# A fused Perceiver block: order of loads and vector work in cross attention, and five value products moved into latent attention's head

## The reference

```python
x = x + cross_attention(layernorm(x), ctx_2048, mask)   # scores over 256 context rows of the same sequence
x = x + latent_attention(layernorm(x), weights)         # 16 heads, low-rank queries (384) and keys/values (128), rotary part (64)
x = x + ffn(layernorm(x), weights)                      # 2048 wide, squared relu, plus one dense "expert" product, layernorm
```

## Time and profile before

| | |
|---|---|
| median of 3 runs | 1130.35 us (1129.69 to 1131.27) |
| the profiled execution | 1130.65 us |
| span of its instructions | 1128.8 us |
| PE busy | 1093.4 us, 97% |
| PEld busy | 950.7 us, 84% |
| DVE busy | 533.0 us, 47% |
| ACT busy | 353.0 us, 31% |
| POOL busy | 323.0 us, 29% |

### The profile page before, as it was taken

One profiled execution on the slowest core, in us unless ns is written; L12 is line 12 of the kernel. 1 busy time (PEld: TensorE's weight loads), 2 busy tenths in 40 slices (PEclk: granted clock), 3 DMA queues, 4 the chain that ended last, 5 costly groups with the idle time before them and its releaser, 6 DMA issues.

```text
span 1128.8 us, 20917 instructions
## 1 busy us (share of the span) xinstructions
PE 1093.4 (97%) x8097; PEld 950.7 (84%) x8097; DVE 533.0 (47%) x998; ACT 353.0 (31%) x699; POOL 323.0 (29%) x370
## 2 busy tenths in 40 slices
PE   5999999999999999999999999999999999999996
PEld 2667686898888888898888888989899998989895
DVE  3666566445344443445344446746254443525242
ACT  3465655232222323232222225513131221213130
POOL 2243362121212112120212122436142332425151
PEclk9899999999999999999999999999999999999998
DMA  9999921101111110201111116501010010101000
GB/s 361 418 420 418 419 91 51 42 20 41 51 42 56 42 46 19 79 19 37 51 42 56 37 49 201 202 1 39 1 38 18 21 38 0 37 0 38 1 19 19
DMA packets 41279, 100.96 MB, mean 89 GB/s; under 512 B 7497, under 2 KB 11620, under 8 KB 36740
## 3 DMA queue, kind: packets, MB, share of 16 engines
q1 hardware_dynamic: 41220, 100.16, 24.7%
HBM read 74.45 MB, written 17.30 MB: 81 GB/s over the span
## 4 chain that ended last, share of the span: by engine, by line
PE 89%; DMA 3%; DVE 3%; issue 2%; POOL 1%; SPq 1%; ACT 1%; DVEq 0%; POOLq 0%; ACTq 0%
PE b_z L44 6%; PE b_z L45 6%; PE b_z L46 6%; PE b_score L44 5%; PE b_prob L44 5%; PE b_prob L46 5%; PE b_score L46 5%; PE b_score L45 5%; PE b_prob L45 5%; PE b_z L1077 3%; PE b_turn L44 2%; PE b_read L608 2%; PE b_read L44 2%; PE b_free L44 2%; PE b_read L46 2%; PE b_free L46 2%
## 5 line engine op out<-in xcount | busy, mean ns | idle before, releaser
L808 POOL TENSOR_TENSOR m_e<-m_e,m_rs 128x512 f32<-128x512 f32 x32 | 34.7, 1085 | 358.2 <-DVE m_rs L955 358.2
L1407 POOL TENSOR_TENSOR f_hT_lo<-f_h,f_hT_hi 128x512 fp32r<-128x512 f32 x64 | 89.6, 1399 | 94.2 <-ACT f_hT_hi L1450 89.5
L46 PE MATMUL b_z<-m_zT_hi,m_wq_hi 128*128 128x256 f32 x384 | 108.7, 283 | 0.0
L44 PE MATMUL b_z<-m_zT_lo,m_wq_hi 128*128 128x256 f32 x384 | 108.7, 283 | 0.0
L45 PE MATMUL b_z<-m_zT_hi,m_wq_lo 128*128 128x256 f32 x384 | 108.7, 283 | 0.0
L1506 DVE TENSOR_TENSOR f_h<-f_h 128x512 f32<-128x512 f32 x64 | 70.6, 1104 | 61.5 <-ACT f_h L1445 61.5
L896 DVE TENSOR_TENSOR m_pT_lo<-b_turn,m_pT_hi 128x512 fp32r<-128x512 f32 x32 | 22.1, 692 | 160.4 <-ACT m_pT_hi L855 160.4
L849 ACT ACTIVATE m_qT<-b_z,m_q_bias 128x256 f32<-128x256 f32 x128 | 53.8, 472 | 79.1 <-PE b_z L46 75.4
L44 PEld LDWEIGHTS b_z<-m_zT_lo,m_wq_hi 128*128 128x128 f32 x384 | 73.7, 192 | 0.0
L45 PEld LDWEIGHTS b_z<-m_zT_hi,m_wq_lo 128*128 128x128 f32 x384 | 73.7, 192 | 0.0
L46 PEld LDWEIGHTS b_z<-m_zT_hi,m_wq_hi 128*128 128x128 f32 x384 | 73.7, 192 | 0.0
(11 more groups left out here) (222 smaller groups left out, 3161.6 us busy)
## 6 DMA issues: line engine op xcount, KB each, us to landing
x_ctx_in<-ctx_rows_dram SPq DMA_DIRECT2D x16, 1024.0 KB, 11.2
x_ctxT<-ctx_turned_dram SPq DMA_DIRECT2D x15, 1024.0 KB, 10.8
m_swapped<-m_by_sin SPq DMA_DIRECT2D x128, 64.0 KB, 2.0
z_scratch<-x_zbuf SPq DMA_DIRECT2D x16, 288.0 KB, 9.7
m_raw<-attn_raw_dram SPq DMA_DIRECT2D x6, 768.0 KB, 11.7
m_z_in<-z_scratch SPq DMA_DIRECT2D x8, 576.0 KB, 3.8
x_x_all<-x_dram SPq DMA_DIRECT2D x16, 256.0 KB, 10.5
x_scratch<-x_x_all SPq DMA_DIRECT2D x16, 256.0 KB, 11.0
```

The costliest lines, as they stand in the source:

```text
L44: nc.tensor.matmul(out, lh, rl, start=first, stop=False)
L46: return nc.tensor.matmul(out, lh, rh, start=False, stop=last)
L808: q.tensor_tensor(e[:], e[:], rs[:].unsqueeze(2).broadcast_to([P, HB, SEQ]), ALU.mult).then_inc(s["normed"], 1)
L1407: g.tensor_tensor(hT_lo[:, 2 * n:2 * n + 2].rearrange("p m n -> p (m n)"), h[:, n % 2], hT_hi[:, 2 * n:2 * n + 2].bitcast(F32).rearrange(" ...
```

## The change

In cross attention:
- x tiles are loaded six ahead instead of four (`XR = 6`): tile 4 directly behind the latent weights, tile 5 behind context 2, and tile p+6 first in slot p. The place of the latent weights among the loads is the same.
- DVE takes the maximum of pair p ahead of the statistics of tile p+2.
- The cast of the latent weights moves from the end of slot 1 to slot 2, behind the copy of the turned probabilities; the split moves to slot 2, behind the maximum and ahead of the statistics.

In the weights and latent attention:
- Of the 16 value products the last five (`LATE`) are made inside the head of latent attention: eight, the turns of the first latents, three more, turn of the keys and rope halves, then unit 0's query products, then three products, then unit 0's scores; two more follow the turn of unit 0's probabilities in unit 1. Their casts and splits go to the same places of ACT and DVE. They use the banks score, prob, read, score, prob; the third waits for the copy of the keys out of read. PE's wait for all 28 fills moves to unit 2; ahead of unit 0 it waits for 23.

```diff
-    XR = 4
+    XR = 6
@@ SP, slot
+            if has(p + 6):
+                load_x(p + 6)
             if has(p + 4):
-                load_x(p + 4)
                 load_ctxT(p + 4)
@@ SP, ahead of slot 0
         sp.dma_start(w_raw[:], A["w_latent"].rearrange("(k p) n -> p k n", p=P)).then_inc(s["w_loaded"], 16)
+        load_x(4)
         load_ctxT(3)
         load_ctx(2)
+        load_x(5)
         sp.dma_start(small[:], A["small"]).then_inc(s["small_loaded"], 16)
@@ ACT, slot
             if has(p - 1):
                 turned_probs(p - 1)
+            if p == 2:
+                act.wait_ge(s["w_loaded"], 16)
+                a.copy(w_hi[:].rearrange(flat), w_raw[:].rearrange(flat)).then_inc(s["w_hi"], 1)
             if has(p + 1):
                 norm(0, p + 1, xn0, x_all[:, p + 1])
...
-            if p == 1:
-                act.wait_ge(s["w_loaded"], 16)
-                a.copy(w_hi[:].rearrange(flat), w_raw[:].rearrange(flat)).then_inc(s["w_hi"], 1)
@@ DVE, slot
+            maximum(p)
+            if p == 2:
+                dve.wait_ge(s["w_hi"], 1)
+                split(w_lo[:].rearrange(flat), w_raw[:].rearrange(flat), w_hi[:].rearrange(flat), s["w_lo"])
             if has(p + 2):
                 first_var(p + 2)
-            maximum(p)
...
-            if p == 1:
-                dve.wait_ge(s["w_hi"], 1)
-                split(w_lo[:].rearrange(flat), w_raw[:].rearrange(flat), w_hi[:].rearrange(flat), s["w_lo"])
@@ PE, slot of latent attention (ACT and DVE alike, with values_hi and values_lo)
                 if runs(g, n):
                     q_unit(g, n, u)
+                if head and u == 0:
+                    for j in range(3):
+                        if j == 2:
+                            pe.wait_ge(s["k_done"], 1)
+                        fill_values(HEADS - w.LATE + j)
+                if head and u == 2:
+                    pe.wait_ge(w.s["lo"], w.FILLS)
                 if runs(g, n, 2):
                     project(*before(2), u - 2, 0)
                 if runs(g, n, 1):
                     turn_probs(u - 1)
+                if head and u == 1:
+                    for j in range(3, w.LATE):
+                        fill_values(HEADS - w.LATE + j)
@@ Weights
+    LATE = 5
     def bank(self, f):
+        late = f - (self.FILLS - self.LATE)
+        if late >= 0:
+            return (self.banks.score, self.banks.prob, self.banks.read, self.banks.score, self.banks.prob)[late]
         return self.banks.ring[f % self.R]
...
-            pe.wait_ge(s["lo"], f - (self.R - 1))
+            late = f - (self.FILLS - self.LATE)
+            pe.wait_ge(s["lo"], f - (self.R - 1) if late < 0 else f - late if late < 3 else f - 2)
@@ PE, ACT and DVE, between the stages (PE's lines)
-            for j in range(12):
+            for j in range(8):
                 w["fill_values"](j)
             m["turn_latent"](0, 0)
             m["turn_latent"](0, 1)
-            for j in range(12, HEADS):
+            for j in range(8, HEADS - weights.LATE):
                 w["fill_values"](j)
...
-            pe.wait_ge(weights.s["lo"], weights.FILLS)
+            pe.wait_ge(weights.s["lo"], weights.FILLS - weights.LATE)
```

More of the change, by code:

```diff
@@ L867, in exp, with slot @@
                 a.activation(e[:], sc[:], ACT.Exp, scale=SCALE).then_inc(s["exped"], 1)
-            def slot(g, n, u):
+            def slot(g, n, u, values_hi):
+                head = isinstance(u, int)
                 if runs(g, n, 1):
@@ L874, in slot @@
                         q_part(n, u, h)
+                if head and u == 0:
+                    for j in range(3):
+                        values_hi(HEADS - w.LATE + j)
                 if runs(g, n, 1):
                     probs(u - 1)
+                if head and u == 1:
+                    for j in range(3, w.LATE):
+                        values_hi(HEADS - w.LATE + j)
                 if n == 3 and has_next(g):
@@ L887, in slot @@
                         keys(g + 1)
-            return dict(latent=latent, keys=keys, groups=lambda: slots(act, slot), exp=exp, q_part=q_part,
+            return dict(latent=latent, keys=keys, exp=exp,
+                        groups=lambda values_hi: slots(act, lambda g, n, u: slot(g, n, u, values_hi)), q_part=q_part,
                         probs=probs, out=out)
@@ L961, in residual, with slot @@
                     v.tensor_tensor(x1[:, j], b_w[j][:], x1[:, j], ALU.add).then_inc(s["x2_done"], 1)
-            def slot(g, n, u):
+            def slot(g, n, u, values_lo):
+                head = isinstance(u, int)
                 if runs(g, n, 1):
@@ L967, in slot @@
                     rotate(n, u)
+                if head and u == 0:
+                    for j in range(3):
+                        values_lo(HEADS - w.LATE + j)
                 if runs(g, n, 1):
@@ L983, in slot, with groups @@
                     mask(u)
-            def groups():
+            def groups(values_lo):
                 dve.wait_ge(s["tables"], 48)
                 dve.wait_ge(s["consts"], 2)
-                slots(dve, slot)
+                slots(dve, lambda g, n, u: slot(g, n, u, values_lo))
             return dict(latent=latent, groups=groups, rotate=rotate, invert=invert, probs=probs, out=out,
@@ L1098, in scores, with slot @@
                 mm.then_inc(s["scored"], 1)
-            def slot(g, n, u):
+            def slot(g, n, u, fill_values):
                 def before(lag):
                     return (g, n - lag) if n >= lag else (g - 1, n - lag + UNITS)
+                head = isinstance(u, int)
                 if runs(g, n):
                     q_unit(g, n, u)
+                if head and u == 0:
+                    for j in range(3):
+                        if j == 2:
[3 more added lines that the diff above has]
+                    pe.wait_ge(w.s["lo"], w.FILLS)
                 if runs(g, n, 2):
@@ L1126, in slot, with groups @@
                     rope_half(*ahead, u + 1, 1)
-            def groups():
-                slots(pe, slot)
+            def groups(fill_values):
+                slots(pe, lambda g, n, u: slot(g, n, u, fill_values))
             return dict(turn_latent=turn_latent, turn_keys=turn_keys, rope_half=rope_half, groups=groups, q_unit=q_unit,
@@ L1727, in _ @@
             act.wait_ge(weights.s["q_bias"], 1)
-            m["groups"]()
+            m["groups"](w["values_hi"])
             f = F["scalar"](act)
@@ L1789, in _ @@
             m["latent"](0, 1)
-            for j in range(12, HEADS):
+            for j in range(8, HEADS - weights.LATE):
                 w["values_lo"](j)
             dve.wait_ge(weights.s["q_bias"], 1)
-            m["groups"]()
+            m["groups"](w["values_lo"])
             f = F["vector"](dve)
```

4 lines of the change are left out of this document (2 added, 2 removed).

## The result

The changed kernel takes **1124.84 us** (median of 12, 1123.77 to 1128.06); beside it on the same chips the kernel before took 1131.29 (1128.84 to 1133.41). The ratio is **0.9951** with a 95% interval of 0.9942 to 0.996: 5.5 us faster, between 4.5 and 6.6. A second chip gave 0.9943 (0.9928 to 0.9957). The two medians lie 6.45 us apart (0.9943); the text goes by the ratio 0.9951, whose interval reaches just beyond that. The forecast was 7.4 us, a ratio of 0.9934. The profiled execution took 1125.78 us, its span 1124.0.

What follows compares the result with a forecast made beforehand. PE, busy for 97% of the span, bounds the kernel, so time comes from its waits and clock. 1130.65 less 1.9 (cross attention) and 5.5 (latent attention) gives 1123.2, as median 1122.9 us; range 1121.0 to 1126.2.

Steps and rivals of the forecast that it cites:

- Loads: Cross attention's start: tile 4, issued directly behind the latent weights, lands 0.6 us after them; the context tiles' delay costs nothing.
- Split in slot 2: Cross attention, slot 2: statistics follow the split without waiting for tile 4; first projection at 30.9, 2.3 us earlier (bounds 1.1, 4.0).
- The clock cost: First projection: PE's clock was 0.50 over its 4.81 us; the forecast left that cost where it was.
- Maximum ahead of statistics: Cross attention, slots 3 to 13: xnT_lo is ready at 51.27, PE arrives at 51.53; 0.26 us to spare, cost nothing.
- The cap: End of cross attention, slot 15: POOL's rotation waits for a z store until 143.66, so at most 1.90 us comes through.
- Five value products: Head of latent attention: 4.29 us leaves the serial stretch; products fill PE's waits, costing 0.06 before scores and 0.1 for the mask.
- first scores at 190.3: Latent attention, unit 0: a predicted sign, PE's first scores starting at 196.45 - 1.9 - 4.24 = 190.3.
- The clock behind the stall: Head of latent attention: filling the 2.36 us idle stretch removes the slow clock behind it, 1.41 us gained.
- Rival 1: Latent attention: the slow clock stays despite the filled hole, 1.41 us less gain, 1124.3 us; chance 11%.

Runs made afterwards that it cites:

- late_only: The value-product part of the change alone (five of the sixteen in the head of latent attention) against the kernel before: 1125.53 against 1130.60 us, ratio 0.9954.
- before_look: One more profiled execution of the kernel before, with nothing changed: 1132.03 us.

## Why the prediction was right, and what it missed

The direction, the two mechanisms and the range (1121.0 to 1126.2) held. By the ratio the size was 1.9 us too large (1.0 by the medians), just beyond the interval of the first chip and inside that of the second.

- **Loads.** Tile 4 landed 0.68 us behind the weights (0.6 forecast). The weights' landing, by contrast, is 22.5 to 24.3 us from execution to execution with the same queue ahead of it, and the first projection moves with it.
- **Split in slot 2.** Forecast 2.3 us at the first projection. Against the landing it is 8.92 less 6.50, 2.42. The two profiles differ by 3.31, because before's landing was 0.9 late. The clock cost was left in place, and it stayed: one stretch at 1.2 GHz falls into the projection in both profiles, which takes 4.81 us in both.
- **Maximum ahead of statistics.** Forecast slack 0.26 us, seen 0.33; cost nothing in eleven slots.
- **The cap.** Forecast: 1.90 come through. Between the profiles it is 2.32 (169.05 to 166.73), with the store landing 0.44 sooner by itself. Over all profiles the first bias product is at 168.60 (five without both parts) and 166.42 us (four with both and the store in its old place): 2.2. Times give 0.8 (0.8 slower to 2.3 faster) for this half.
- **Five value products.** Forecast 4.29 less 0.16. From the bias products to the first scores before took 27.40 us, late_only 23.26: 4.14. The 0.15 us lost lies ahead of the scores, where the sum had 0.06: it took the hole as 2.51 us, and the bracket of its own row says 2.36. The prediction's first scores at 190.3 came at 191.68 because the clock fell at 170.
- **The clock behind the stall.** Forecast 1.41 gained. The six profiles with the idle times take 40.15 us on average from unit 0's to unit 3's q products, and a filled one 38.8; the one without a slow stretch 38.65. So 1.50 in the mean, 1.35 of it left after the two small leftovers: the term holds as a mean, though single executions gave 0 to 2.9. Rival 1, which came from the Trainium skill's advice on longer gaps (TensorE: Matmul & The Clock Gate, "Why this matters for your kernels"), is refuted by measurement here: with gaps of 2.36 and 1.79 us five of six profiles have a slow stretch, with the gaps filled none of eight.
- **What the sum left out.** The weak step is its frame: it took the granted clock of one profile for the kernel's. It credited a slow stretch where that profile had one and had no term for the places where it could have had one. Behind the bias products the profiles with both cross-attention parts lose: mean 22.80 us to the q products (five products of 4.29 added where they had moved) against 20.90 in the five others, **1.9 us**. The forecast 7.4 less that is 5.5, the gain by the ratio. That it fits to a tenth is partly luck, as cross attention gave 2.2 instead of 1.90 and another place was left out too. Behind the first down product, for which PE waits 2.7 us, the clock fell in six of the twelve profiles with that wait (none of them before's two), and the rest of PE's work then took 384.1 us in the mean instead of 382.3; it fell in neither of the two with 1.07 us. That the slow clock is there is shown; why it is there more often isn't.

In the changed kernel's profile the books close as follows: first bias product 2.32 us sooner, then 2.61 (4.29 less 1.68), then 1.35, nothing up to the down products (505.21 and 505.23), and 1.35 lost again behind them, where the clock fell at 730: 4.91 in sum, against 4.8 of the spans.

## What to carry to other kernels

Take more than one profile before you put a price on a clock stretch, and list each place where PE is idle for about 2 us or makes a row of one-column matmuls as one where it may fall; its cost over many executions is about a frequency times a price. When DMA is full, a gain at the head can be capped by a buffer whose store stands behind a large load, as here: look for a store that lands at the same time whatever the engines do, and issue it ahead of that load. Before work is taken out of one piece, look what it covers.

## What the runs showed of the hardware

- A matmul with one column keeps PE "busy" (3.63 us for 32), and yet the clock fell to 1.2 GHz during or within 1.5 us behind them in 7 of 11 profiles, and in none of the three where value products stood between. A full busy row is no promise of 2.4 GHz.
- The same program at the same place may or may not fall: before and before_look differ in two of five places. This hangs together with what the Trainium skill says (TensorE: Matmul & The Clock Gate, "What's actually happening"): the monitor runs on its own and doesn't start with the kernel.
- The same DMA issued in the same order landed up to 1.8 us apart between executions (the weights at 22.45 to 24.29 in twelve profiles, issued at 6.4 to 7.4), which is as much as the whole effect of this half of the change.
- The gap ahead of the first down product, marked "issue", is POOL's: PE starts 0.1 us after its subtraction of 128 x 512. That takes 1.30 us where DVE is idle (at 702 us), 1.28 beside DVE's multiplication, which itself grows from 0.68 to 1.57, and 3.05 beside DVE's weight splits:

```profile
722.99 1.28 POOL L1441 TENSOR_TENSOR f_hT_lo<-f_h,f_hT_hi 128x512 fp32r<-128x512 f32 x1
725.56 3.05 POOL L1441 TENSOR_TENSOR f_hT_lo<-f_h,f_hT_hi 128x512 fp32r<-128x512 f32 x1 [1.28 <-ACT f_hT_hi L1484]
```
